# The output projection as plain fp32: eight matmuls a tile step instead of twenty-four

## What is computed

```python
# x: (4, 1024, 256), context: (4, 154, 256), 16 heads of 16
q, k, v = ...                       # projections, rotary positions
attn = softmax(q @ k.T) @ v         # per head
attn = attn.reshape(B, H, T, D).transpose(0, 2, 1, 3).reshape(B, T, E)
return attn @ Wo.T + bo             # the output projection
...
x = x + jnp.tanh(g_xattn[0]) * _L0_xattn_ref(_layernorm(x, axis=-1), ctx_1024, ctx_1024, ...)
x = x + jnp.tanh(g_ffn[0]) * _L0_ffn_ref(_layernorm(x, axis=-1), ...)
```

## Time and profile before

| | us |
|---|---|
| median of 3 runs | 604.42 |
| lowest and highest | 602.23 and 604.69 |
| the profiled execution's own time | 603.83 |
| its span, first to last instruction | 602.0 |
| mean granted clock of TensorE, share of full speed | 0.946 |

### The profile page before, as it was taken

One profiled execution on the slowest core, in us unless ns is written; L12 is line 12 of the kernel. 1 busy time (PEld: TensorE's weight loads), 2 busy tenths in 40 slices (PEclk: granted clock), 3 DMA queues, 4 the chain that ended last, 5 costly groups with the idle time before them and its releaser, 6 DMA issues.

```text
span 602.0 us, 8537 instructions
## 1 busy us (share of the span) xinstructions
PE 524.9 (87%) x3360; PEld 400.0 (66%) x3360; DVE 416.3 (69%) x960; ACT 238.3 (40%) x389; POOL 84.9 (14%) x121
## 2 busy tenths in 40 slices
PE   2668864999989998999989998999899999989795
PEld 1545454855977487856976497738885697649574
DVE  4667355867989478958888488867896578644423
ACT  3252514363354624454335424452436343442210
POOL 2426012011110112011201121011201110101000
PEclk9865975999999999999999999999999999999798
DMA  7301010010101000011002010101002000200000
GB/s 265 112 2 36 2 35 2 0 49 1 37 0 44 31 35 2 37 48 35 1 1 73 1 35 1 66 19 36 1 4 70 0 2 1 73 1 1 2 35 36
DMA packets 6132, 18.50 MB, mean 31 GB/s; under 512 B 932, under 2 KB 1772, under 8 KB 5964
## 3 DMA queue, kind: packets, MB, share of 16 engines
q10 hardware_dynamic: 4005, 12.53, 6.0%
q1 hardware_dynamic: 2087, 5.42, 2.7%
HBM read 13.49 MB, written 4.19 MB: 29 GB/s over the span
## 4 chain that ended last, share of the span: by engine, by line
PE 71%; DVE 16%; ACT 8%; issue 3%; POOL 1%; DMA 1%; ACTq 0%; DVEq 0%
PE psF L1112 17%; PE psF L1052 11%; PE psX L1099 6%; ACT probs L521 4%; PE psX L988 4%; PE psX L1158 4%; PE psX L970 4%; DVE max_t L733 4%; PE psO L1172 3%; PE psF L1172 3%; PE psF L1175 3%; PE psO L1175 3%; PE psF L1058 2%; PE psX L1085 2%; DVE h_lo L726 2%
## 5 line engine op out<-in xcount | busy, mean ns | idle before, releaser
L733 DVE TENSOR_REDUCE max_t<-psX 128x4 fp32r<-128x616 f32 x128 | 99.8, 795 | 6.0 <-PE psX L1099 3.0
L521 ACT ACTIVATE probs<-psX 128x1024 f32<-128x1024 f32 x64 | 63.8, 1024 | 50.5 <-PE psX L1158 50.5
L1112 PE MATMUL psF<-w_hi,h_hi 128*128 128x284 f32 x256 | 76.8, 300 | 2.4 <-DVE h_lo L726 1.5
L1112 PE MATMUL psF<-w_lo,h_hi 128*128 128x284 f32 x256 | 75.2, 294 | 0.0
L1112 PE MATMUL psF<-w_hi,h_lo 128*128 128x284 f32 x256 | 74.9, 293 | 0.0
L1099 PE MATMUL psX<-km,qT 96*128 96x308 f32 x256 | 65.2, 341 | 7.1 <-DVE max_t L733 3.6
L1099 PEld LDWEIGHTS psX<-km,qT 96*128 96x128 f32 x256 | 48.7, 204 | 23.8 <-DVE max_t L733 12.1
L431 ACT ACTIVATE h_hi<-psF 128x512 fp32r<-128x512 f32 x64 | 37.3, 594 | 63.0 <-PE psF L1058 63.0
L726 DVE SCALAR_TENSOR_TENSOR h_lo<-psF,h_hi 128x512 fp32r<-128x512 f32 x64 | 43.7, 685 | 15.7 <-ACT h_hi L431 15.7
L1112 PEld LDWEIGHTS psF<-w_hi,h_hi 128*128 128x128 f32 x256 | 48.2, 188 | 7.8 <-issue 4.6
L311 POOL TENSOR_TENSOR x<-x,tab 128x256 f32<-128x256 f32 x32 | 22.3, 730 | 206.3 <-DMA x<-in_x_dram 206.3
(11 more groups left out here) (155 smaller groups left out, 990.2 us busy)
## 6 DMA issues: line engine op xcount, KB each, us to landing
x<-in_x_dram ACTq DMA_DIRECT2D x8, 512.0 KB, 3.3
x_ln<-in_x_dram ACTq DMA_DIRECT2D x7, 512.0 KB, 3.3
out_dram<-x ACTq DMA_DIRECT2D x7, 512.0 KB, 2.6
heads_t<-in_w_dram SPq DMA_DIRECT2D x1, 1024.0 KB, 8.5
heads_t<-in_w_dram SPq DMA_DIRECT2D x1, 994.0 KB, 4.6
tab<-in_tables_dram SPq DMA_DIRECT2D x1, 674.0 KB, 7.0
x_ln<-in_x_dram SPq DMA_DIRECT2D x1, 512.0 KB, 3.4
wkv_sb<-in_wkv_dram SPq DMA_DIRECT2D x1, 512.0 KB, 9.8
```

The source lines that it names most:

```text
L521: nc.scalar.activation(dst, psX[:, 2 * (i % 2):2 * (i % 2) + 2, :], ACT.Exp).then_inc(sc_exp.sem, 1)
L733: V.tensor_reduce(max_t[:, k, half, :].rearrange("p (h g) -> p g h", h=2)[:, 2 * j:2 * j + 2, :], psX[:, 2 * j:2 * j + 2, 0:2 * S].rearran ...
L1112: ins = mm(psF[:, F_OF_K[k], 0:W2N], a[:, m, tokens(k)], w[:, m, :], start=m == 0 and i == 0, stop=m == HT - 1 and i == 2)
```

## The change

`project_out` takes the transposed heads `o_t` and the weights `wo_sb` as they are, in plain F32: two matmuls for each of the four row blocks, 8 in all, in place of 24. The tiles `oT_hi`, `oT_lo`, `wo_hi`, `wo_lo` go, and with them `heads_high` on ACT, `head_low` on DVE, the copy of `wo` on ACT and its subtraction on POOL. `wo` is loaded by one DMA straight into `wo_sb`. TensorE waits for `o_back` instead of `o_hi` and `o_lo`. The ACT wait for `wo_ps` ahead of q_hi stays.

```diff
-        wo_hi, wo_lo = (sb(f"wo_{n}", [P, 2, E], F32R) for n in ("hi", "lo"))
+        wo_sb = sb("wo_sb", [P, 2, E])
...
-            stage("wo", wo)
+            sp.dma_start(wo_sb[:, :, :], wo.rearrange("p (f e) -> p f e", f=2)).then_inc(wo_loaded.sem, 16)
...
-                    for n in ("wo", "lora1", "lora2"):
+                    for n in ("lora1", "lora2"):
                         stage_low(n)
...
-            def heads_high(c, f2):
-
-                act.wait_ge(o_back.sem, o_back.at(c, f2 + 1))
-                copy(oT_hi[:, f2, :], o_t[:, f2, 1, :]).then_inc(o_hi.sem, 1)
...
-            def head_low(c, f2):
-                dve.wait_ge(o_hi.sem, o_hi.at(c, f2 + 1))
-                V.tensor_tensor(oT_lo[:, f2, :], o_t[:, f2, 1, :], oT_hi[:, f2, :].bitcast(F32),
-                                ALU.subtract).then_inc(o_lo.sem, 1)
...
                 if second:
-                    pe.wait_ge(w_lo["wo"].sem, 1)
-                pe.wait_ge(o_hi.sem, o_hi.at(d))
-                pe.wait_ge(o_lo.sem, o_lo.at(d))
+                    pe.wait_ge(wo_loaded.sem, 16)
+                pe.wait_ge(o_back.sem, o_back.at(d))
                 for k in range(TT):
                     o_ps = psX[:, k // 2, E * (k % 2):E * (k % 2) + E]
-                    n = 0
-                    for a, w in ((oT_hi, wo_hi), (oT_lo, wo_hi), (oT_hi, wo_lo)):
-                        for f in range(2):
-                            ins = mm(o_ps, a[:, f, tokens(k)], w[:, f, :], start=n == 0, stop=n == 5)
-                            n += 1
+                    for f in range(2):
+                        ins = mm(o_ps, o_t[:, f, 1, tokens(k)], wo_sb[:, f, :], start=f == 0, stop=f == 1)
```

More of the change, by code:

```diff
@@ L83, in build @@
         qs = split[:, :].rearrange("p (k g r) -> p k g r", k=TT, g=NG)
-        oT_hi = split[:, 0:2 * CH].rearrange("p (f t) -> p f t", f=2)
-        oT_lo = split[:, 2 * CH:4 * CH].rearrange("p (f t) -> p f t", f=2)
         heads_t = sb("heads_t", [P, NQ, 16, 32])
@@ L169, in build @@
         wkv_loaded = count("wkv_loaded", 16)
-        w_loaded = {n: count(f"{n}_loaded", 16) for n in ("wq", "wo", "w1", "w2a", "w2b", "lora1", "lora2")}
+        wo_loaded = count("wo_loaded", 16)
+        w_loaded = {n: count(f"{n}_loaded", 16) for n in ("wq", "w1", "w2a", "w2b", "lora1", "lora2")}
         a1_loaded = count("a1_loaded", 16)
@@ L195, in build @@
         den_inv, o_norm = count("den_inv", 2), count("o_norm", 2)
-        o_back, o_hi, o_lo = count("o_back", 2), count("o_hi", 2), count("o_lo", 2)
+        o_back = count("o_back", 2)
         wo_ps, x1_s = count("wo_ps", 2), count("x1_s", 2)
@@ L220, in build @@
         n_w2 = (HT - 1) * W2N
-        staged = {"wq": q6, "wo": x1_1[:, 0:2 * E], "w1": flat_h, "w2a": flat_h[:, 0:n_w2],
+        staged = {"wq": q6,  "w1": flat_h, "w2a": flat_h[:, 0:n_w2],
                   "w2b": q6[:, 0:W2N], "lora1": x1_0[0:LR, :], "lora2": q7[0:LR, 256:256 + E]}
@@ L225, in build @@
         halves = {n: [t[:, :, :].rearrange("p a b -> p (a b)") for t in pair] for n, pair in
-                  {"w1": (w1_hi, w1_lo), "wo": (wo_hi, wo_lo), "w2": (w2_hi, w2_lo),
+                  {"w1": (w1_hi, w1_lo), "w2": (w2_hi, w2_lo),
                    "wq": (wq_hi, wq_lo)}.items()}
@@ L381, in reload @@
                 else:
-                    n = "wo" if u else "lora1"
-                    act.wait_ge(w_lo[n].sem, 1)
+                    if not u:
+                        act.wait_ge(w_lo["lora1"].sem, 1)
                 act.dma_start(x1[:, u], x_d[b, u]).then_inc(x1_loaded[u].sem, 16)
@@ L500, in step @@
                 else:
-                    for n in ("wo", "lora1", "lora2", "w2a", "w2b"):
+                    for n in ("lora1", "lora2", "w2a", "w2b"):
                         stage_high(n)
@@ L525, in step @@
                         ctx_copy(b + 1)
-                for f2 in range(2):
-                    heads_high(c, f2)
             stage_high("wq")
@@ L806, in step @@
                 q_sine(c, u)
-                if not first:
-                    head_low(d, 1)
                 q_sum(c)
@@ L865, in step @@
                 head_blocks(c, 2)
-                head_low(c, 0)
                 if not last:
```

## The result

The changed kernel has a median of 605.51 us against 604.29 us for the kernel before (19 runs each), a ratio of 1.0028 with a 95% interval of 1.0015 to 1.0041. So it is slower by 1.2 us between the medians, and by 0.9 to 2.5 us by the interval: a real difference, inside the 0.5% that the prediction counted as no change. The forecast was 606.5, range 603.0 to 609.2, with no change as the likeliest case. The profiled execution took 605.40 us, its span is 603.6.

A forecast was written before the change was run, and what follows sets the result against it. The prediction took TensorE's unbroken chain as the bound, with seven of eight projections paid in full. It summed 603.83 + 4.8 - 2.4 = 606.2, then carried half of a 0.59 median offset to 606.5 us, range 603.0 to 609.2.

The forecast's parts named there:

- The bound: Projections of steps 2 to 7 and the tail lie in full on TensorE's path, with no slack beside them.
- the term for the edges: In each new projection, 0.10 us at its end and some 0.05 at its start, added to 3.42 for 16 records.
- +0.69: Added us for each full-clock projection: 3.57 in the new form against 2.88 before.
- +4.8: Added us for the seven projections of steps 2 to 7 and the tail, 7 x 0.69.
- rival 2: Edges at each of a projection's four accumulation groups, 0.265 us a record: 611.6 us, chance 0.06.
- The four passes: Trainium skill rule that true fp32 needs four array passes; at 0.12 each, 0.48 us a matmul, 3.84 a projection.
- rival 3: Each fp32 matmul costs four passes of 0.12 us, 3.84 a projection: 608.3 us, chance 0.08.
- The removed work: Copies on ACT and subtractions on DVE in full steps, and staging of `wo` in step 0: worth 0 us.
- Step 1: The one gain: projection starts 2.03 us earlier, no longer waiting for the subtraction; taken as -2.4 us.
- Half clock for 3.0 us: Clock case chosen for the projection of step 1, then full clock: 5.05 us, end at 87.5, gain 2.4.
- rival 1: Step 1's gain given back by half clock in its projection (608.2 us) or an unmoved later rise (607.4); chance 0.24.
- rival 4: Faster or level: step 1's projection at full clock (604.7 us) and an earlier later rise, up to 3 more (601.7); chance 0.12.

The follow-up runs named there:

- k5: The changed kernel run again unaltered, beside the kernel before on another chip: 604.80 against 603.93 us, ratio 1.0014.
- k7: The kernel before with the plain fp32 projection in step 1 alone, the other seven split: 600.70 against 603.93 us, ratio 0.9955.
- k2: The changed kernel with copies and subtractions put back and awaited by TensorE, so only the matmul format differs from before: 608.04 against 603.29 us, ratio 1.0084.
- k6: The changed kernel with head copies and subtractions put back, awaited by nobody, repeated beside k5: 605.00 us, ratio to before 1.0026.
- k1: The changed kernel with head copies and subtractions put back, awaited by nobody, first run: 606.72 against 603.29 us, ratio 1.0054.
- k8: The changed kernel with 11 unused matmuls on TensorE ahead of the projection of step 1: 604.00 against 603.93 us, ratio 1.0012.
- k3: The changed kernel with every projection done twice into the same place: 634.18 us, one execution.
- k11: k10 with 13 unused matmuls ahead of the projection of step 1 and 30 behind, part of the result still dropped: 597.75 us, ratio to before 0.9909.
- k4: The kernel before with every projection done twice into the same place: 624.29 us, one execution.
- k9: k7 with 11 unused matmuls ahead of the projection of step 1 and 30 behind: 597.49 against 603.37 us, ratio to before 0.9902.
- k10: The kernel before with each projection's 16 high-part matmuls first, part of the result dropped: 600.07 against 603.37 us, ratio 0.9940.
- k12: k10 with one start mark for each PSUM bank, so the whole result is computed: 600.39 against 603.81 us, ratio to before 0.9946.

## Why the prediction was right

**The bound.** Seven of eight projections are paid in full: 3.45 in the chain for 2.87 or 2.88 in all seven, with no new slack. From step 3 to step 4 the query projections are 67.03 apart for 66.46, 0.57 more, and two other steps are 0.57 and 0.59 longer; in k5 the two steps between them are 0.65 and 0.68 longer, in the changed kernel's first profile 1.46 (its half-clock stretch) and 0.94. k7 confirms it with times, 4.1 us for the seven, and k2, whose 4.8 is 4.0 and 0.7 of step 1, agrees.

**The price was 0.12 too high.** The step that missed is the term for the edges: 3.42 + 0.10 + 0.05 = 3.57. The records are 0.216 apart, not 0.213 (the last digit of two rows), which makes 3.45 for 16, and the edges of the short groups of the earlier trace rows don't show here; doubling the work doubles the time, 6.91 for 3.45. So +0.69 was +0.57, and +4.8 was +4.0. What rival 2's 0.265 holds above 0.216 is edges alone: its chance was put low for the right reason.

**The four passes.** A matmul of 0.431 is four times 0.108. The prediction priced a pass by a whole F32R matmul, 0.12, which made rival 3's 3.84. The rule of the Trainium skill ("FP8 and Floating Point Precision", "TensorE Precision Notes"), four passes for true fp32, agrees with the trace if a pass is priced at 0.108; the trace itself shows two records a matmul, not four. The Trainium skill's "TensorE: Matmul & The Clock Gate", "Back-to-back issue gap", gives the gap of a matmul on its own at full clock as its columns over 2.4 GHz plus 2.5 ns. By that an estimate for 256 columns is 0.107 and 0.0025, so 0.109: the fp32 passes come out at that or just under it, and the F32R matmul, 0.12 in the trace, 0.011 above it.

**The removed work.** Taken as 0, found as 0 for the copies and subtractions of the heads (k6 beside k5: 67.09 and 67.04 a step). The staging of the weights in step 0 was taken as 0 too; no run has it apart.

**Step 1.** The projection starts 0.14 behind the last transpose, where the sum had 0.03. The value taken for it, 5.05, lay between the 5.39 of the first profile and the 3.71 of k5; both are within the bounds of 3.57 and 7.1. Half clock for 3.0 us was 3.4 (83.2 to 86.6), so the projection ended at 88.04 and not at 87.5: by itself a gain of 1.9, not of 2.4. What was not in the sum is what follows: it had nothing behind the projection, and rival 1 had half of the gain lost if the later rise keeps its moment. The rise came sooner instead, at 100.2 for 106.8, and added 1.7, so that the gain was 3.6 in that execution; by the medians of k7 it was about 3.2. That is half of rival 4, its later rise, with 1.7 of the up to 3 us that it was given. Its other half, a projection at full clock, happens too, in the profiles of k5 and k6. Rival 4 was given 0.12; in the profiles of the fp32 form it is no rare case.

**What was luck.** The two errors, 0.8 too much cost and 0.8 to 1.2 too little gain, both point the same way. Together they put the time 1.6 to 2.0 under the forecast, and it came 1.0 under. From the median before, 604.29 + 4.0 - 3.2 = 605.1, 0.4 below the 605.51 found, which the interval covers. Stray half-clock stretches (step 3 here, others elsewhere) may fill the rest. Between 110 and 550 us five of the seven profiles with fp32 in every projection have one or two (the changed kernel, k1, k2, k6, k8; not k3, k5), and two of the seven with split projections there (k7, k11; not the kernel before, k4, k9, k10, k12). No run separates whether that is the format's doing. So the mechanism of the seven places was right with its price a fifth too high, and step 1, where the clock varies from execution to execution, was a middle value that happened to lie near.

## What to carry to other kernels

Compare formats by the distance between starts, not by counts of matmuls: a third of the instructions cost 20% more time here (3.45 for 2.88). A change whose cost falls on every repetition and whose gain falls on the one place where an engine waits for its operands should be split: the gain was had alone, by the new form in that place or by taking first what was ready first (k7, k12). Where TensorE stands for microseconds ahead of dense work, unused matmuls in the gap can be worth more than the change under study (k9).

## What the runs showed of the hardware

- A plain fp32 matmul of 256 columns costs 0.431 us at full clock, in two records of 0.216, and an F32R one 0.12: 3.6 times, so three F32R matmuls are cheaper by 0.07.
- A wait of TensorE of 2.7 us left the clock alone in the profiles of k5 and k6 and came with half clock in those of the changed kernel, k1, k3 and k7: in k3 from 81.2 on, 1.9 us after the values ended, in the changed kernel from 83.2 on, when TensorE had been at work again for 0.5 us. With the 4.7 us of the kernel before, of k2 and of k4 it fell each time.
- Half clock behind a wait of 7.6 us lasts on into work: 93.4 to 100.2 in the changed kernel, 93.1 to 106.8 in the one before. How long varies between executions: 10.2 us in k5 and k2, 13.7 in k12. Filling the wait removed it in k9, whose clock stayed full from 60 us, in the scores of step 0, to 552 us, in the tail.
